# Key-weight fold, weight preparation and last Gram stores moved in a two-stage delta-rule block

## The reference

```python
def ref(x):                                      # x: [32, 512, 256]
    x = x + attn(layernorm(x))                   # outer residual 1
    x = x + ffn(layernorm(x))                    # outer residual 2
def attn(x):
    x = x + delta(LN(x, dn_g, dn_b));  return x + relu(LN(x, mn_g, mn_b) @ w1 + b1) @ w2 + b2
def delta(x):
    q, k, v = split(x @ gates_w + gates_b);  lr = x @ lr_w + lr_b
    k = k / norm(k);  A = tril(k k^T, -1) + I
    u = solve_triangular(A, v)
    return (q k^T) (lr * u) @ out_w + out_b
def ffn(x):                                      # int32 weights, scaled by 1/127
    return (silu(x @ wg.T) * (x @ wu.T)) @ wd.T  # hidden size 768
```

## Time and profile before

| | |
|---|---|
| median of 3 runs | 1669.64 us (1667.93 to 1669.79) |
| the profiled execution | 1668.0 us, its span 1666.3 us |
| PE busy | 1605.2 us, 96% |
| DVE, POOL, ACT busy | 1126.5, 813.5, 774.9 us |
| mean granted clock of TensorE | 0.986 |
| DMA | 178.19 MB, mean 107 GB/s |

### The profile page before, as it was taken

One profiled execution on the slowest core, in us unless ns is written; L12 is line 12 of the kernel. 1 busy time (PEld: TensorE's weight loads), 2 busy tenths in 40 slices (PEclk: granted clock), 3 DMA queues, 4 the chain that ended last, 5 costly groups with the idle time before them and its releaser, 6 DMA issues.

```text
span 1666.3 us, 29768 instructions
## 1 busy us (share of the span) xinstructions
PE 1605.2 (96%) x10622; PEld 1444.2 (87%) x10622; DVE 1126.5 (68%) x2711; ACT 774.9 (47%) x1501; POOL 813.5 (49%) x1176
## 2 busy tenths in 40 slices
PE   6999998699999999999999999999999999999997
PEld 5999997588889998888899988888899999999986
DVE  5667773377777766777776677777776666666663
ACT  4667663144444444444444444444444444444442
POOL 5556772244444444444444454444444444444441
PEclk9999999699999999999999999999999999999998
DMA  6988888112222232222222312222223222222200
GB/s 184 362 279 289 296 299 274 55 58 70 69 69 73 72 107 68 69 66 66 66 79 72 114 55 70 65 68 64 79 75 102 73 78 71 72 70 70 69 13 26
DMA packets 148587, 178.19 MB, mean 107 GB/s; under 512 B 77781, under 2 KB 130264, under 8 KB 140248
## 3 DMA queue, kind: packets, MB, share of 16 engines
q1 hardware_dynamic: 148440, 176.28, 32.1%
HBM read 98.64 MB, written 77.59 MB: 106 GB/s over the span
## 4 chain that ended last, share of the span: by engine, by line
PE 70%; DVE 8%; issue 2%; POOL 2%; ACT 1%; POOLq 0%; DVEq 0%; ACTq 0%
PE ps L167 28%; PE ps L1053 18%; PE ps L1063 10%; PE ps L973 6%; PE ps L984 4%; PE ps L967 4%; DVE a L1457 1%; DVE bs L1462 1%; DVE late L1326 1%; DVE x2a L1302 1%; DVE bs L1316 1%; POOL sc L1484 1%; DVE xn L1309 1%; ACT late L1172 0%; DVE wt L1286 0%
## 5 line engine op out<-in xcount | busy, mean ns | idle before, releaser
L1531 POOL TENSOR_TENSOR hl<-late,hh 128x512 fp32r<-128x512 f32 x128 | 166.3, 1299 | 212.2 <-ACT hh L1177 212.2
L1063 PE MATMUL ps<-wdT,hh 128*128 128x256 f32 x768 | 204.0, 302 | 8.4 <-ACT late L1172 8.2
L1177 ACT ACTIVATE hh<-late 128x512 fp32r<-128x512 f32 x192 | 120.8, 629 | 180.2 <-DVE late L1326 180.2
L1181 ACT ACTIVATE z_hi<-ps 128x256 fp32r<-128x256 f32 x128 | 48.9, 382 | 306.3 <-PE ps L984 306.3
L1063 PE MATMUL ps<-wdT,hl 128*128 128x256 f32 x768 | 187.0, 281 | 2.0 <-DVE hl L1331 2.0
L1326 DVE TENSOR_TENSOR late<-ps,late 128x512 f32<-128x512 f32 x192 | 132.5, 690 | 67.0 <-PE ps L1053 64.2
L1172 ACT ACTIVATE late<-ps 128x512 f32<-128x512 f32 x192 | 113.6, 592 | 126.0 <-PE ps L1053 126.0
L1510 POOL TENSOR_TENSOR xhm_lo<-xh,xhm_hi 128x1024 fp32r<-128x1024 f32 x32 | 76.5, 2390 | 169.1 <-DVE xhm_hi L1396 169.1
L1063 PEld LDWEIGHTS ps<-wdT,hh 128*128 128x128 f32 x768 | 144.9, 189 | 13.2 <-ACT late L1172 10.8
L1053 PE MATMUL ps<-xh3T_hi,wgT 128*128 128x512 f32 x384 | 154.7, 403 | 0.7 <-DVE xh3T_lo L1331 0.7
L1053 PE MATMUL ps<-xh3T_lo,wgT 128*128 128x512 f32 x384 | 152.7, 398 | 0.0
(11 more groups left out here) (215 smaller groups left out, 4770.7 us busy)
## 6 DMA issues: line engine op xcount, KB each, us to landing
xhT_scratch<-xhTk SPq DMA_DIRECT2D x32, 1024.0 KB, 6.5
xhT<-xhT_scratch SPq DMA_DIRECT2D x32, 1024.0 KB, 6.4
gg_scratch<-late SPq DMA_DIRECT2D x32, 640.0 KB, 3.7
gg<-gg_scratch SPq DMA_DIRECT2D x32, 640.0 KB, 3.9
xk<-in_L_attn_x_dram SPq DMA_DIRECT2D x32, 512.0 KB, 5.5
xt<-in_L_attn_x_dram SPq DMA_DIRECT2D x32, 512.0 KB, 4.1
out_dram<-late SPq DMA_DIRECT2D x32, 512.0 KB, 2.9
low_scratch<-late SPq DMA_DIRECT2D x128, 16.0 KB, 2.3
```

The lines of the kernel that those rows point to most:

```text
L1063: mm = pe.matmul(ps[:, (FG, FU)[j // 2], (j % 2) * C:(j % 2 + 1) * C], part[:, h, blk(j)], wdT[:, h, :], start=(h == 0 and part is hh), st ...
L1177: act.activation(hh[:, h, :], hf[:, h % 2, :], ACT.Copy).then_inc(hh_ev[h], 1)
L1531: pool.tensor_tensor(hl[:, h, :], hf[:, h % 2, :], hh[:, h, :].bitcast(F32), ALU.subtract).then_inc(hl_ev[h], 1)
```

## The change

- The key weights are only scaled (`wg`) and transposed. The shift is made as a column (`kcol`, one value for each output channel) by matmuls with one moving column, and added by ACT as the bias of its eviction of the transposes. The two columns of the rate get their shift apart (`lrow`, `wlr`).
- `mv` is double, and `stats(n)` waits for the norms of n - 2. On DVE the rate's columns and statistics 2 come ahead of the split of S.
- PREP is 8. The nine FFN steps leave the keys stage. In round 0 of the main stage PE does four transposes behind each of nine steps of the attention, into the four banks that round 0 leaves free, and ACT evicts them between its own steps.
- The buffers `xn`, `xa2` and the two `x2` of the main stage now share memory with the FFN's integer weights, which live on into round 0; PE, ACT and POOL wait at round 1 for the transposes.
- The stores of the last Gram matrix are issued by SP in the main stage, ahead of the loads of sequence 1.

```diff
@@ setup_dve
-                dve.wait_ge(shift_done, 1)
                 for k in range(CB):
-                    dve.scalar_tensor_tensor(out=wfold[:, k, :], in0=wall[:, k, :], scalar=dcol[:, 0, k:k + 1],
-                                             in1=shift[:, :], op0=ALU.mult, op1=ALU.add).then_inc(fold_done, 1)
+                    dve.tensor_scalar(wg[:, k, :], wall[:, k, 0:C], dcol[:, 0, k:k + 1], None, ALU.mult).then_inc(wg_done, 1)
+                dve.wait_ge(kcol_ps, 1)
+                dve.tensor_scalar(kcol[:, :], ps[:, P0, 0:CB], 1.0 / C, None, ALU.mult).then_inc(kcol_done, 1)
@@ setup_act
-                act.wait_ge(shift_ps, 1)
-                act.activation(shift[:, :], ps[:, P0, 0:KW], ACT.Copy, scale=1.0 / C).then_inc(shift_done, 1)
                 act.wait_ge(wkT_ps, 1)
-                act.activation(wkT[:, :, :], ps[:, G0, :].rearrange("p (k c) -> p k c", c=C), ACT.Copy).then_inc(wkT_ev, 1)
+                act.wait_ge(kcol_done, 1)
+                for o in range(CB):
+                    act.activation(wkT[:, o, :], ps[:, G0, o * C:(o + 1) * C], ACT.Identity, scale=1.0,
+                                   bias=kcol[:, o:o + 1]).then_inc(wkT_ev, 1)
@@ setup_pe
-                pe.wait_ge(diff_bc_done, CB)
-                for k in range(CB):
-                    pe.matmul(ps[:, P0, 0:KW], diff_bc[:, k, :], wall[:, k, :], start=(k == 0), stop=False)
-                pe.matmul(ps[:, P0, 0:KW], ones[0:1, :], brow[:, :], start=False, stop=True).then_inc(shift_ps, 1)
+                pe.wait_ge(diff_done, 1)
+                for o in range(CB):
+                    for k in range(CB):
+                        pe.matmul(ps[:, P0, o:o + 1], wall[:, k, o * P:(o + 1) * P], diff[:, k:k + 1], start=(k == 0), stop=False)
+                    mm = pe.matmul(ps[:, P0, o:o + 1], brow[:, o * P:(o + 1) * P], ones[0:1, 0:1], start=False, stop=True)
+                mm.then_inc(kcol_ps, 1)
...
+                for k in range(CB):
+                    pe.matmul(ps[:, P0 + 1, 0:2], diff_bc[:, k, :], wall[:, k, C:KW], start=(k == 0), stop=False)
+                pe.matmul(ps[:, P0 + 1, 0:2], ones[0:1, :], brow[:, C:KW], start=False, stop=True).then_inc(lrow_ps, 1)
@@ store_gram
-                sp.wait_ge(g_act, n + 1)
-                sp.wait_ge(g_dve, n + 1)
+                if n < NS - 1:
+                    sp.wait_ge(g_act, n + 1)
+                    sp.wait_ge(g_dve, n + 1)
@@ stats
-                wait(dve, ln_done, n)
+                wait(dve, ln_done, n - 1)
@@ keys_dve
                 stats(dve, 1)
+                setup_lr(dve)
+                stats(dve, 2)
                 setup_s(dve)
                 dve_xhT(dve, 0)
-                setup_lr(dve)
-                stats(dve, 2)
@@ prep_*
-            PREP = 6
+            PREP = 8
@@ finish_sp
-                for n in range(NS - 2, NS):
-                    store_gram(sp, n)
+                store_gram(sp, NS - 2)
@@ main stage, PE
+                def pe_weights(pe, i, f):
+                    if i > 0:
+                        return
+                    wait(pe, wt_ev, f + 1 - len(FREE))
+                    for b in range(4):
...
+                        mm = pe.transpose(ps[:, FREE[f % len(FREE)], blk(b)], src, ident[:, :])
+                    mm.then_inc(wt_ps, 1)
@@ pe_body: behind levels 1 to 4, z 3, z 2, z 1, z 0, and the last step of B^T
+                        pe_weights(pe, i, 0)
...
+                        pe_weights(pe, i, 8)
@@ act_body
+                    act_weights(act, i, range(0, 4))
                     if att:
                         act_z(act, i, 3)
+                    act_weights(act, i, (4,))
...
                         act_z(act, i, 2)
+                        act_weights(act, i, (5,))
@@ main stage, SP
                     sp.dma_start(lanes[0][:, :], low_slot[1]).then_inc(lanes[3], 16)
+                    store_gram(sp, NS - 1)
```

More of the change, by code:

```diff
@@ L139, in delta_block_kernel @@
         ggk = [late[:, 3 * q:3 * q + 3, :].rearrange("p a b -> p (a b)")[:, 0:GW] for q in range(2)]
+        work = sb("work", [P, 3 * HB * C])
+        x2s = [work[:, q * TB * C:(q + 1) * TB * C].rearrange("p (j c) -> p j c", c=C) for q in range(2)]
+        xa2, xn = (work[:, q * TB * C:(q + 1) * TB * C].rearrange("p (j c) -> p j c", c=C) for q in (2, 3))
+        wgf, wuf = (work[:, q * HB * C:(q + 1) * HB * C].rearrange("p (h c) -> p h c", c=C) for q in range(2))
+        wdf = work[:, 2 * HB * C:3 * HB * C].rearrange("p (k h) -> p k h", h=H)
+        wgi, wui, wdi = wgf.bitcast(I32), wuf.bitcast(I32), wdf.bitcast(I32)
         gg_out = [ctx.enter_context(nc.semaphore(f"gg_out{q}")) for q in range(2)]
@@ L250, in delta_block_kernel @@
             diff_bc = sb("diff_bc", [P, CB, P], c=pre)
-            shift = sb("shiftk", [P, KW], c=pre)
-            wfold = sb("wfoldk", [P, CB, KW], c=pre)
+            wg = sb("wgk", [P, CB, C], c=pre)
+            kcol = sb("kcol", [P, CB], c=pre)
+            lrow = sb("lrow", [P, 2], c=pre)
+            wlr = sb("wlr", [P, CB, 2], c=pre)
             wkT = sb("wkT", [P, CB, C], c=pre)
@@ L341, in setup_pe @@
                 pe.wait_ge(ones_set, 1)
+                pe.wait_ge(diff_done, 1)
[4 more added lines that the diff above has]
+                mm.then_inc(kcol_ps, 1)
+                pe.wait_ge(id_done, 1)
+                pe.wait_ge(wg_done, CB)
+                for o in range(CB):
+                    for k in range(CB):
+                        mm = pe.transpose(ps[:, G0, o * C + k * P:o * C + (k + 1) * P], wg[:, k, o * P:(o + 1) * P], ident[:, :])
+                mm.then_inc(wkT_ps, 1)
                 pe.wait_ge(diff_bc_done, CB)
                 for k in range(CB):
-                    pe.matmul(ps[:, P0, 0:KW], diff_bc[:, k, :], wall[:, k, :], start=(k == 0), stop=False)
-                pe.matmul(ps[:, P0, 0:KW], ones[0:1, :], brow[:, :], start=False, stop=True).then_inc(shift_ps, 1)
-                pe.wait_ge(id_done, 1)
-                pe.wait_ge(fold_done, CB)
-                for o in range(CB):
-                    for k in range(CB):
-                        mm = pe.transpose(ps[:, G0, o * C + k * P:o * C + (k + 1) * P], wfold[:, k, o * P:(o + 1) * P], ident[:, :])
-                mm.then_inc(wkT_ps, 1)
-                pe.wait_ge(wkT_ev, 1)
+                    pe.matmul(ps[:, P0 + 1, 0:2], diff_bc[:, k, :], wall[:, k, C:KW], start=(k == 0), stop=False)
+                pe.matmul(ps[:, P0 + 1, 0:2], ones[0:1, :], brow[:, C:KW], start=False, stop=True).then_inc(lrow_ps, 1)
+                pe.wait_ge(wkT_ev, CB)
                 for m in range(CB):
@@ L727, in prep_dve @@
                     dve.tensor_copy(dst[:, :, :], src[:, :, :]).then_inc(ints_f, 1)
-                if FFN_AT < q <= FFN_AT + len(whole):
-                    n = q - FFN_AT - 1
+                if SPLIT_AT < q <= SPLIT_AT + len(whole):
+                    n = q - SPLIT_AT - 1
                     w, (hi, lo), _, _ = whole[n]
@@ L771, in prep_act @@
                     act.activation(four(wqk[:, :, :].rearrange("p a b -> p (a b)")), pieces, ACT.Copy).then_inc(qk_done, 1)
[L772 to L778, removed]
+                if SPLIT_AT <= q < SPLIT_AT + len(whole):
+                    w, (hi, lo), made, n = whole[q - SPLIT_AT]
                     if made is not None:
@@ L829, in prep_pe @@
                     mm.then_inc(qk_ps, 1)
[L830 to L840, removed]
             with nc.Block() as block:
@@ L931, in delta_block_kernel @@
             fo_ps, ot_ev = sems("fo_ps", 2), sems("ot_ev", 2)
+            wt_ps, wt_ev = sem("wt_ps"), sem("wt_ev")
+            FFN_STEPS = 3 * HB * CB // 4
+            FREE = (FG, FU, FO0, FO1)
             def diag(j):
@@ L1194, in act_relu, with act_weights @@
                     act.activation(dst[:, m, :], ps[:, (FU, S0)[m], :], ACT.Relu, bias=b1f[:, m:m + 1]).then_inc(done[m], 1)
+                def act_weights(act, i, steps):
+                    for f in steps if i == 0 else ():
+                        dst = (wgT, wuT, wdT)[f // 3][:, :, :].rearrange("p a b -> p (a b)")
+                        act.wait_ge(wt_ps, f + 1)
+                        act.activation(dst[:, f % 3 * 4 * P:(f % 3 + 1) * 4 * P], ps[:, FREE[f % len(FREE)], :],
+                                       ACT.Copy).then_inc(wt_ev, 1)
                 def act_body(act, i, att, mlp, down, m, r):
+                    if i == 1:
+                        act.wait_ge(wt_ps, FFN_STEPS)
                     if mlp:
@@ L1489, in pool_body @@
                 def pool_body(pool, i, att, mlp, down, m, r):
+                    if i == 1:
+                        pool.wait_ge(wt_ps, FFN_STEPS)
                     if mlp:
```

56 lines of the change are left out of this document (35 added, 21 removed).

## The result

The changed kernel takes 1655.68 us (median of 4 runs, 1654.79 to 1656.42) against 1669.72 for the kernel before, a ratio of 0.9918 with a 95% interval of 0.9901 to 0.9935. The profiled execution took 1655.95 us with a span of 1654.2, which is 12.1 us less span than before. Five marks in the two time lines divide it.

A forecast was written before the change was run, and what follows sets the result against it. PE bounds the keys stage, except at the start, seam and first main sequence. Terms -4.0 - 2.3 - 1.9 + 1.0 - 0.2 = -7.4 us take 1668.0 to 1660.6, plus 1.64 for the median: 1662.2 us; range 1658.0 to 1665.6.

The forecast's parts named there:

- Step 1: Keys stage: nine FFN transposition steps leave it, each costing 0.44 us on PE; -4.0 us.
- Step 2: Seam between keys and main stage: last Gram stores issued behind it, so DVE arrives last; -2.3 us.
- Step 3: Start of keys stage: S 1.5 us sooner, PE leads by 2.8 at the first Gram, shrinking to 1.5-2.8; -1.9 us.
- Rival B: Keys stage's first 75 us: DMA sets the end, start gives nothing; group 7 and levels cost upper bounds; 1665.5 us, chance 0.18.
- The sign that was to tell: Keys stage, sequence 9: a lead under 1 us there would show the forecast wrong.
- Step 4: Main stage's sequence 0: nine groups of FFN transposes in PE's gaps, partly sticking out; +1.0 us (0 to 2.2).
- rival A: Sequence 0: transposes lift PE's clock early; some 5 us less, 4 counted; 1658.2 us, chance 0.12.
- The small term beside it: Sequence 0's first level: shorter seam idle can leave PE at the fast clock, four cases in ten; -0.2 us.
- C: Keys stage: another resource paces sequences without a step at 8.0 us, start gives nothing; 1668.3 us, chance 0.06.
- D: Sequence 0: transposes and evictions join the chain, 13.7 us against 8.2 gained; 1675.1 us, chance 0.04.

The follow-up runs named there:

- the start alone: The kernel before with only the start of the change (key weights folded as a bias, double mean and variance, new DVE order): 1666.48 us, 1.0001.

## Why the prediction was wrong

**Step 1, the FFN steps, held.** In the changed kernel PE's lead grows from 1.52 us at sequence 16 to 4.17 at sequence 22, 0.44 for each of the six steps in between, as forecast.

**Step 2, the stores, held.** Seam 3.73 to 1.34 us, -2.4 against -2.3; alone 0.9987.

**Step 3, the start.** The chain was right, but for ACT's table load, which cost 0.5 us of it: S at 13.0 (forecast 13.2), the lead at the first Gram 3.4 (forecast 2.8). The step that failed is "DMA's own lead is only the 1.5 us [...] so the lead shrinks to between 1.5 and 2.8". It took no account of x of sequence 5 standing behind twelve loads, whose issue alone keeps SP from 24.8 to 32.7: between sequences 3 and 7 the stretch takes back 1.0 to 3.4 us of a lead of 3.4 to 4.3, by execution. In the profile after nothing was left; in the second one of the same kernel 2.2 us. That the twelve loads cause the stall at sequence 5 rests on the two kernels with them spread, which lose nothing; the start alone, with the twelve in place, had its 1.0 us of loss only before sequence 7, and why it differs stays open. Rival B named the mechanism; its zero was true of one profile and of the ten executions of the start alone. Only one of the ten has a trace, so it stays open why their median shows next to nothing where that trace leads by 3 us. The sign that was to tell, a lead under 1 us at sequence 9, could not: the weight steps begin two sequences later, and the lead there is 5.4 us for that reason.

**Step 4, the transposes, had the right cost and the wrong consequence.** What sticks out of the gaps can be read where the clock is slow, in the second profile of the changed kernel: the levels start 2.72, 2.67, 2.62 and 2.49 us apart (the last is z 3), against 2.72, 2.67, 2.49 and 2.34 in the earlier trace rows: 0, 0, 0.13 and 0.15, forecast 0, 0.1, 0.2 and 0.3. The step that failed is "the sum takes that it does not": the forecast left the clock at the slow level with PE nearly without a gap. It was rival A that happened, and it gave more than its price. Where +0.8 us was forecast for round 0, it became 5.6 to 7.6 us shorter in the two profiles, and the two rounds together 4.8 to 6.6. The part that rival A priced, from the first level to z 1, gave 5.1 us in the first profile (18.8 to 13.7) and 1.7 in the second (17.1), where the clock came back later; A had "some 5 us less" and counted 4. E and M, which it left out, gave 2.3 in both. The rows of before left the question open, as the prediction says; what spoke against A was the rule that the fast clock does not engage for transposes (the Trainium skill, "TensorE: Matmul & The Clock Gate", part 4). For these fp32 transposes between matmuls the traces do not agree with it: the useless ones alone made round 0 8.4 us shorter, at a mean granted clock of 0.91 instead of 0.65. Whether transposes with no matmuls between them would raise the clock was not run. The small term beside it, a fast first level in four cases of ten, was fairly put: four of the nine traces with the short seam have one.

**The cases.** Rival A had 0.12; with its 1658.2 it also set the lower end of the range, and since it came larger the result fell 2.3 us below it, although the start gave less than forecast: the two misses stand against each other. C and D did not occur: the steps are worth 0.44 us each, and round 0 hid the evictions. The direction was right, at 0.88.

## What to carry to other kernels

In a stretch that is a chain of small steps across engines, as round 0 is here, work moved into PE's gaps had a second effect beside its own cost: it decided at which clock the matmuls of the chain ran. Price a move of PE work at both clocks, take the two as the ends of the range, and try it with useless instructions in the gaps before moving anything. A lead won at the start is worth only what the next transfers let through: look up which load stands behind which, in SP's order, and spread the ones that nobody waits for. Trace the same kernel more than once before giving a number to one round: here one round differed by up to 3.4 us between executions of the same instructions.

## What the runs showed of the hardware that was not expected

Four useless 128x128 transposes in each gap of a chain of levels, 36 in all, take round 0 from 46.1 to 37.7 us, with the mean granted clock of the round going from 0.65 to 0.91. The 36 FFN transposes in later gaps leave the levels slow, and E and M fast. Two executions of one kernel, with the same seam of 1.3 us, start the first level at different clocks (1.17 and 1.99 us) and differ by 1.9 us in round 0: a part of the scatter between executions is the clock. A load of 512 KB whose landing took 5.4 us in the median of this execution landed 8.3 us behind its issue when it stood behind twelve weight loads (issue at 32.76, DVE's start on it at 41.06); in the trace of the start alone it was 6.6 us (31.99, 38.62).
